# Reciprocals of the softmax sums by way of DRAM and GpSimd in the final stage of a transformer layer

## The reference, cut to what matters

```
probs = softmax(where(mask, -inf, q k^T / sqrt(32) + attention_bias))   # per head
ctx   = probs @ v                                # heads side by side: [tokens, 512]
x     = x + (ctx @ Wo + bo)
h     = layernorm(x) * g2 + beta2
x     = x + gelu2(h @ W1 + b1) @ W2 + b2         # gelu2(t) = t * sigmoid(1.702 t)
out   = rotate(x)                                # groups of 4 columns by angles theta, phi
```

## Time and profile before

| | us |
|---|---|
| median of 3 runs (3502.69 to 3505.73) | 3504.41 |
| the profiled execution: its time | 3502.99 |
| its span, first to last instruction | 3501.3 |
| its first two stages with their drain, to about | 2438 |
| its eight super-tiles, from 2476.05 to the end | 1025 |

### The profile page before, as it was taken

One profiled execution on the slowest core, in us unless ns is written; L12 is line 12 of the kernel. 1 busy time (PEld: TensorE's weight loads), 2 busy tenths in 40 slices (PEclk: granted clock), 3 DMA queues, 4 the chain that ended last, 5 costly groups with the idle time before them and its releaser, 6 DMA issues.

```text
span 3501.3 us, 60955 instructions
## 1 busy us (share of the span) xinstructions
PE 3415.7 (98%) x18338; PEld 1940.2 (55%) x18338; DVE 2486.0 (71%) x4176; ACT 1885.6 (54%) x2541; POOL 2084.9 (60%) x646
## 2 busy tenths in 40 slices
PE   8999799999999999999999999998899999999998
PEld 3444466666666666666666666665344444444443
DVE  5666599999999999999999999997434333343331
ACT  3222388888888888888888888886111111111110
POOL 0000499999899999999998999996202201211100
PEclk9999899999999999999999999999999999999999
DMA  8999999999999999999999999999402211210100
GB/s 290 340 338 339 360 365 349 344 348 351 399 344 348 350 350 345 394 352 349 351 343 367 378 351 347 346 351 324 107 19 54 72 32 40 72 51 21 48 12 12
DMA packets 288702, 906.20 MB, mean 259 GB/s; under 512 B 93344, under 2 KB 93344, under 8 KB 211360
## 3 DMA queue, kind: packets, MB, share of 16 engines
q1 hardware_dynamic: 240272, 811.43, 64.8%
q10 hardware_dynamic: 45840, 86.00, 7.0%
q0 software_dynamic: 2560, 8.39, 0.6%
HBM read 763.12 MB, written 142.61 MB: 259 GB/s over the span
## 4 chain that ended last, share of the span: by engine, by line
PE 86%; DVE 1%; DMA 1%; issue 0%; ACT 0%; SPq 0%; POOL 0%; DVEq 0%; ACTq 0%
PE b_T L765 27%; PE bank_ctx L788 14%; PE scores L731 14%; PE scores L1309 13%; PE b_T L1320 9%; PE bank_ctx L1320 3%; PE scores L1290 3%; PE scores L737 1%; DMA penb<-in_L_cond_b 1%; PE scores L1250 0%; PE scores L1299 0%; PE b_T L1326 0%; DVE probT L1151 0%; PE scores L1264 0%; ACT penb L1049 0%
## 5 line engine op out<-in xcount | busy, mean ns | idle before, releaser
L590 POOL TENSOR_TENSOR ring<-ring,penb 128x1856 f32<-128x1856 f32 x512 | 1904.5, 3759 | 502.1 <-DMA penb<-pen_scratch 416.8
L685 ACT ACTIVATE ring<-ring,low 128x2048 f32<-128x2048 f32 x512 | 1028.9, 2010 | 318.1 <-DVE low L654 318.1
L765 PEld LDWEIGHTS b_T<-ident,ring 128*128 128x128 f32 x8192 | 889.3, 141 | 434.2 <-DVE probT L638 430.8
L765 PE MATMUL b_T<-ident,ring 128*128 128x128 f32 x8192 | 1091.1, 276 | 6.5 <-DVE probT L638 5.9
L654 DVE CUSTOM_DVE_ANT_0 ring<-scores,ring 128x1024 f32<-128x1024 f32 x512 | 627.1, 1225 | 177.0 <-PE scores L731 153.8
L638 DVE COPY probT<-b_T 128x512 f32<-128x512 f32 x1024 | 702.0, 686 | 3.9 <-PE b_T L765 3.8
L654 DVE CUSTOM_DVE_ANT_0 ring<-scores,ring,low_part 128x1024 f32<-128x1024 f32 x512 | 652.6, 1275 | 0.4
L731 PE MATMUL scores<-keys,queries 128*128 (+1 forms) x2048 | 621.1, 424 | 21.1 <-DMA queries<-q_rows 16.7
L788 PE MATMUL bank_ctx<-probT,values 128*32 128x512 f32 x4096 | 546.2, 605 | 0.1
L695 ACT COPY probT<-b_T 128x512 f32<-128x512 f32 x1024 | 537.7, 575 | 0.2 <-PE b_T L765 0.2
L1016 POOL TENSOR_TENSOR keys_again<-keys_again,values 128x512 f32<-128x512 f32 x32 | 40.4, 1263 | 779.1 <-DVE values L1239 779.1
(11 more groups left out here) (131 smaller groups left out, 1930.9 us busy)
## 6 DMA issues: line engine op xcount, KB each, us to landing
ring<-in_fside_Bx16xSxS SPq DMA_DIRECT2D x512, 1024.0 KB, 7.4
keys<-k_rows SPq DMA_DIRECT2D x64, 1024.0 KB, 8.5
values<-v_heads ACTq DMA_DIRECT2D x128, 256.0 KB, 6.2
queries<-q_rows SPq DMA_DIRECT2D x128, 256.0 KB, 8.0
ctx_scratch<-ctxp ACTq DMA_DIRECT2D x128, 256.0 KB, 6.6
penb<-ctx_scratch SPq DMA_DIRECT2D x120, 256.0 KB, 4.7
k_rows<-part_hi SPq DMA_DIRECT2D x64, 256.0 KB, 3.3
k_rows<-part_lo SPq DMA_DIRECT2D x64, 256.0 KB, 3.4
```

Source lines behind the costliest of these rows:

```text
L590: nc.gpsimd.tensor_tensor(ring[:, j, 0:POOL_MASKED], ring[:, j, 0:POOL_MASKED], penb[:, j, 0:POOL_MASKED], ALU.add).then_inc(masked, 1)
L685: nc.scalar.activation(ring[:, k, :], ring[:, k, :], ACT.Exp, bias=low[:, k:k + 1], scale=-1.0, accum_out=column(sums_all, trip, k)).then_ ...
L765: last = nc.tensor.transpose(turn_bank(slot, n)[:, c * P:(c + 1) * P], ring[:, slot, at:at + P], ident[:])
```

## The change

From super-tile 1 on the reciprocals are no longer widened on ScalarE, turned on PE and multiplied on VectorE. All reciprocals of group 0 (super-tiles 0 and 1) are made before step 0 of the drain, those of the other three groups once, at `front(1, 1)`. PE turns them in 1 and 3 transposes, ScalarE copies the result over `low_all` and stores it to a new DRAM tensor `recip_scratch` (`keep_rows`). SP loads them with each piece as rows spread over 32 partitions each (`load_per_row`, one more DMA of 256 KB a piece), and GpSimd multiplies (`context`). GpSimd starts on super-tile 1 when the four tiles of super-tile 0 are normalised (`first_hn`). Super-tile 0 keeps the old way.

Beside that: bo is loaded in the place of g2, and g2 with beta2 and b2; VectorE waits for bo alone before the sums with it, and for the other rows after all four pieces and these sums; b2 is added to super-tile 0 at f = 2, 3, 9 and 13 of the first feed-forward; the three `sem_inc` stand ahead of `first_front`.

```diff
+        after(-1)
         for j in range(R):
             step(TRIPS, j)
             after(j)
...
+        def load_per_row(to, group, half, c, signal):
+            sp.dma_start(to, recip_scratch[bass.ds(group * H + 4 * c, 4), bass.ds(half * TOK, TOK)]
+                         .rearrange("h (o n) -> h o n", o=1).to_broadcast([4, DH, TOK])).then_inc(signal, 16)
...
-        sp.dma_start(g2_all, row(g2)).then_inc(vec_in, 16)
+        sp.dma_start(bo_all, row(bo)).then_inc(bo_in, 16)
...
         after_scores(7)
+        sp.dma_start(b2_all, row(b2)).then_inc(vec_in, 16)
+        sp.dma_start(g2_all, row(g2)).then_inc(vec_in, 16)
         sp.dma_start(beta2_all, row(beta2)).then_inc(vec_in, 16)
-        sp.dma_start(bo_all, row(bo)).then_inc(vec_in, 16)
-        sp.dma_start(b2_all, row(b2)).then_inc(vec_in, 16)
...
                 load_parts(parts[:, c % 2], v, c, part_ld[c % 2])
+                load_per_row(per_row[:, c % 2], v // 2, v % 2, c, part_ld[c % 2])
...
+        sp.wait_ge(recip_stored[0], 16)
+        load(1)
+        sp.wait_ge(recip_stored[1], 16)
+        with sp.Fori(2, NU) as v:
...
+        def context(v, c):
+            pool.wait_ge(part_ld[c % 2], (v - 1) * 160 + (c // 2) * 80 + 80)
             add_parts(parts[:, c % 2], v, c)
+            pool.wait_ge(summed, v * DB + c + 1)
+            if c == 0:
+                pool.wait_ge(wo_done, v * QT)
+            nc.gpsimd.tensor_tensor(ctxT[:, c, :], parts[:, c % 2, 0, :], per_row[:, c % 2], ALU.mult).then_inc(ctxT_ready, 1)
...
+        pool.wait_ge(first_hn, QT)
         for c in range(DB):
-            parts_of(1, c)
+            context(1, c)
...
+    def keep_rows(act, recip_rows, first, count, n):
+        act.wait_ge(recip_turned, n)
+        nc.scalar.copy(of_groups(low_all, first, count), recip_rows[:, first * GC:(first + count) * GC]).then_inc(recip_copied, 1)
+        act.wait_ge(recip_copied, n)
+        act.dma_start(recip_scratch[first * H:(first + count) * H, :].rearrange("(g h) (j q) -> (h j) g q", h=H, q=P),
+                      of_groups(low_all, first, count).rearrange("p (g q) -> p g q", q=P)).then_inc(recip_stored[n - 1], 16)
...
         if j == 3:
-            widen(act, 0, 2)
-            widen(act, 0, 3)
+            keep_rows(act, up[0], 0, 1, 1)
+            widen(act, 2)
+            widen(act, 3)
...
+            if isinstance(v, int) and v == 1 and f == 4:
+                keep_rows(act, fore[0], 1, GROUPS - 1, 2)
...
-            context(0)
-            context(1)
-            dve.wait_ge(vec_in, 80)
-            nc.vector.tensor_scalar(b1_scaled[:], b1_col[:], 1.702, None, ALU.mult).then_inc(consts_ready, 1)
+            for c in range(DB):
+                context(c)
+            dve.wait_ge(bo_in, 16)
             dve.wait_ge(xm_ld, 16)
-            for t in range(2):
-                nc.vector.tensor_tensor(xm_in[:, t, :], xm_in[:, t, :], bo_all, ALU.add)
-            context(2)
-            context(3)
-            for t in range(2, QT):
+            for t in range(QT):
                 last = nc.vector.tensor_tensor(xm_in[:, t, :], xm_in[:, t, :], bo_all, ALU.add)
             link(last)
+            dve.wait_ge(vec_in, 64)
+            nc.vector.tensor_scalar(b1_scaled[:], b1_col[:], 1.702, None, ALU.mult).then_inc(consts_ready, 1)
...
-            for t in range(QT):
-                last = nc.vector.tensor_tensor(x2[:, 0, t, :], x2[:, 0, t, :], b2_all, ALU.add)
-            link(last)
...
+            if isinstance(v, int) and v == 1 and f in (2, 3, 9, 13):
+                first_residual((2, 3, 9, 13).index(f))
+            if isinstance(v, int) and v == 1 and f == 1:
+                divisors(dve, fore[1], 1, GROUPS - 1, 2)
...
-        first_front()
-        dve.sem_inc(c_chain, LINKS - 1)
+        dve.sem_inc(c_chain, LINKS)
         dve.sem_inc(hid_ready, 4)
         dve.sem_inc(acc_read, 4)
+        first_front()
...
         def front(v, f):
-            if 1 <= f <= DB:
-                c = f - 1
-                pe.wait_ge(wide_ready, v * DB + c + 1)
-                if c < 2:
-                    need(pe, hT_ready, v * DB - 1 + c)
-                else:
-                    pe.wait_ge(ctxT_ready, v * DB + c - 1)
-                turn_recip(pe, v, c, fore[c % 2])
-            elif 5 <= f < 9:
+            if isinstance(v, int) and v == 1:
+                if f == 3:
+                    turn_recip(pe, fore[0], 1, GROUPS - 1, 2)
+                if f == 5:
+                    pe.wait_ge(recip_copied, 2)
+            if 5 <= f < 9:
```

More of the change, by code:

```diff
@@ L481, in __init__ @@
     def __init__(self, ring, penb, probT, keys, queries, values, scores, bankT, bank_ctx,
-                 masked, scored, added, turned, pv_done, ctx_copied, ctx_stored, SCORED0, TURNED0, PV0):
+                 masked, scored, added, exp_done, turned, pv_done, ctx_copied, ctx_stored, SCORED0, TURNED0, PV0):
         self.ring, self.penb, self.probT = ring, penb, probT
@@ L485, in __init__ @@
         self.scores, self.bankT, self.bank_ctx = scores, bankT, bank_ctx
-        self.masked, self.scored, self.added, self.turned = masked, scored, added, turned
+        self.masked, self.scored, self.added, self.exp_done, self.turned = masked, scored, added, exp_done, turned
         self.pv_done, self.ctx_copied, self.ctx_stored = pv_done, ctx_copied, ctx_stored
@@ L805, in phase_b, with phase_c @@
                     Left(ring, penb, probT, keys_again, queries_again, values, scores, bankT, bank_ctx,
-                         masked, scored, added, turned, pv_done, ctx_copied, ctx_stored, SCORED0, TURNED0, PV0))
-def phase_c(nc, sem, ctx, left, ctx_scratch, xm_scratch, Wo, bo, W1, b1, W2, b2, g2, beta2, out, ident, trig, sums_all, low_all):
+                         masked, scored, added, exp_done, turned, pv_done, ctx_copied, ctx_stored, SCORED0, TURNED0, PV0))
+def phase_c(nc, sem, ctx, left, ctx_scratch, xm_scratch, Wo, bo, W1, b1, W2, b2, g2, beta2, out, ident, trig, sums_all, low_all,
+            recip_scratch):
     CH = 2
@@ L1089, in scalar, with divisors @@
         supertiles(act, ffn, front, nothing)
[L1091 to L1096, removed]
+    def divisors(dve, undefined, first, count, n):
+        cols = slice(first * GC, (first + count) * GC)
+        sums = of_groups(sums_all, first, count)
+        nc.vector.tensor_scalar(undefined[:, cols], of_groups(low_all, first, count), 2.0, 0.0, ALU.mult, ALU.mult)
+        nc.vector.reciprocal(sums, sums).then_inc(recip_chain, 1)
+        dve.wait_ge(recip_chain, n)
+        nc.vector.tensor_tensor(sums, sums, undefined[:, cols], ALU.add).then_inc(recip_ready, 1)
     def vector_between(dve, j):
-        if j == 0:
-            divisors(dve, 0)
+        if j == -1:
+            dve.wait_ge(left.added, TRIPS * R * CH)
+            divisors(dve, fore[1], 0, 1, 1)
     def vector(dve):
-        LINKS = 7
+        LINKS = 6
         def first_front():
@@ L1174, in front @@
                     last = nc.vector.tensor_tensor(xm_in[:, t, :], xm_in[:, t, :], bo_all, ALU.add)
[L1175 removed]
+                link(last, 1)
             if 5 <= f < 9:
@@ L1184, in front @@
                     last = nc.vector.bn_stats(stats[:, t, :], x2_v[:, t, :])
-                link(last, 3)
+                link(last, 2)
                 dve.nop(nofuse=True)
@@ L1240, in late, with turn_recip @@
                 last.then_inc(rotated, 1)
[L1242 to L1243 removed]
+        dve.sem_inc(c_chain, LINKS)
         dve.sem_inc(hid_ready, 4)
         dve.sem_inc(acc_read, 4)
+        first_front()
         supertiles(dve, ffn, front, late)
[L1248 to L1250 removed]
+    def turn_recip(pe, recip_rows, first, count, n):
+        pe.wait_ge(recip_ready, n)
+        for g in range(first, first + count):
+            last = nc.tensor.transpose(recip_rows[:, g * GC:(g + 1) * GC], of_groups(sums_all, g, 1), ident[:])
         last.then_inc(recip_turned, 1)
     def tensor_between(pe, j):
+        if j == 2:
+            turn_recip(pe, up[0], 0, 1, 1)
         if j in (2, 4):
[L1256 removed]
+            if j == 4:
+                pe.wait_ge(recip_copied, 1)
             for c in (j - 2, j - 1):
                 pe.wait_ge(wide_ready, c + 1)
[L1259 removed]
+                for t in range(QT):
+                    last = nc.tensor.transpose(first_fore[c][:, t * P:(t + 1) * P], first_wide[:, c % 2, t, :], ident[:])
+                last.then_inc(wide_turned, 1)
     def tensor(pe):
```

84 lines of the change are left out of this document (37 added, 47 removed).

## The result

The changed kernel takes 3468.52 us (median of 4 runs, 3466.98 to 3469.0), the kernel before 3504.49 us: 36.0 us less, ratio 0.9897 with a 95% interval of 0.988 to 0.9914. The forecast was 3467 us. The profiled execution took 3466.98 us with a span of 3465.3 us, against 3502.99 and 3501.3.

What follows compares the result with a forecast made beforehand. PE was taken as the bound inside the super-tiles, a chain of loads, VectorE work and a semaphore at the join; 3502.99 - 23.3 - 14.1 = 3465.6 us, plus 1.4 for the runs' median, gave 3467 us, range 3461 to 3477.

Steps and rivals of the forecast that it cites:

- clock at the first up-products: First feed-forward stretch after PE's idle time: the 3.1 us loss to the lower clock stays, 0 change.
- Part 1: Super-tiles: 28 sets of reciprocal transposes (L1250) and PE's waits go, three transposes are added; 23.3 us less.
- Part 2: GpSimd's pieces are ready before PE's product with Wo at f = 5: 7.5 us ahead, 13 at super-tile 1; cost 0.
- two reloads of 5 to 6 us: Super-tile 1: two reloads, beside three GpSimd pieces of 5.3 us, bring GpSimd to about 2487, PE needing them at 2500.
- Part 3: Drain ends 3 to 4 us earlier; GpSimd's last sum, 2435.3, is late next; product with Wo over at 2439.5 to 2441.2.
- Part 4: Join: rows land at 2441.94 and release the first sum after Wo at 2442.2, not 2449.83; 7.6 us less.
- Part 5: End of preparation: sums with b2 leave the path, PE starts at 2461.95 behind ScalarE's copies; 6.5 us less.
- (a): Rival at the join: only part is gained, as W1 or rows land late or the drain ends no earlier; 3 to 10 us, chance 0.20.
- (b): Rival in the super-tiles: VectorE and GpSimd hold each other up, 7 to 14 us come back; chance 0.10.
- (c): Rival at f = 5 of seven super-tiles: GpSimd becomes the bound and the kernel slower, 3512 us or more; chance 0.03.
- (d): Rival: new waits replace those removed in the super-tiles and loads still bound the join; 3500 to 3508 us, chance 0.03.

Runs made afterwards that it cites:

- the loop alone: Changed kernel with the join put back as before (row loads, sums with b2, semaphore increments): 3479.81 us, 24.5 us below the kernel before.
- GpSimd's order: Changed kernel with GpSimd summing, and VectorE multiplying, super-tile 0's pieces in load order (0, 2, 1, 3): 3468.59 us.
- n = 3: Changed kernel with three extra GpSimd multiplications, results unused, in each piece of super-tiles 2 to 7: 3470.25 us.
- n = 6: Changed kernel with six extra GpSimd multiplications, results unused, in each piece of super-tiles 2 to 7: 3527.41 us.
- the two runs on the increments: Kernel before with the three semaphore increments moved ahead of super-tile 0's preparation: 3502.57 us; the same with GpSimd held back by the `first_hn` wait: 3499.76 us.
- the last kernel: Changed kernel with rows loaded ahead of W1, GpSimd's sums in load order, and W2's second half loaded behind super-tile 1's loads: 3463.7 us.
- the increments alone: Kernel before with only the three semaphore increments moved ahead of super-tile 0's preparation: 3502.57 us, ratio 0.9992.
- both orders: Changed kernel with rows b2, g2, beta2 loaded ahead of W1's first half and GpSimd's super-tile 0 sums in load order: 3468.18 us.

## Why the prediction was right

The forecast, 3467 us, missed by 1.5 us. Its terms, in the profiled executions:

| step | predicted | measured |
|---|---|---|
| sets of L1250 and their waits, less three transposes | 23.3 | 23.3 |
| clock at the first up-products | 0 | 1.1 |
| first sum after Wo | 7.6 | 5.15 |
| sums with b2 and the increments | 6.5 | 6.5 |
| sum | 37.4 | 36.0 |

The first row is 24.4 less 1.1. (Worked out without the clock: from the second super-tile's feed-forward to the last one's, six starts, they were 128.74 us apart on the mean and are 125.36. Seven times the difference, less 0.33 us for the three new transposes, is 23.4.) The 1.1: 16 matmuls of the first up-products took 9.87 us before, where 6.87 is their length at full clock, 3.0 us lost; now 24 took 12.24 in place of 10.3, 1.9 us lost. The third is 2449.83 less 2444.68 (7.6 was worked out from 2442.2); the fourth is 26.22 us from there to PE's start, before, less 19.74.

**Part 1** held to 0.1 us, and the loop alone shows it by itself (23.2 us behind PE's start): what stood in PE's own queue was won whole, and nothing took its place.

**Part 2** held for super-tiles 2 to 7: ready at T + 25.9, T + 26.9 foretold, 8.4 us to spare, 7.5 foretold. The run with 7.6 us of extra work stands just at the threshold, the one with 15.2 us far beyond it. For super-tile 1 its size was wrong: 13 us foretold, 1.9 us measured. The step that failed is "two reloads of 5 to 6 us": they took 10.3 and 11.8 us. The nearest row was a single DMA's landing (4.6 us), not that of five DMAs one after the other, 1.25 MB, of which the last has to land. The second also ran beside 1 MB of input rows. It cost nothing in this kernel, and 5.5 to 5.7 us in the two runs that changed GpSimd's order and left W2 where it was: 3.5 to 3.8 us of waiting, and 1.9 us of clock in the product behind.

**Part 3** was right on the drain (4.7 us earlier, 3 to 4 foretold) and on what is late next, GpSimd's last sum. But that sum ended at 2437.2, not 2435.3, so that the product started at 2438.05, not 2436.1, and I had 5.1 us as the product's worst, from the earlier trace rows; it took 6.6. A longer idle time isn't the reason: PE had stood 4.62 us before it, and 6.50 us in the kernel before, where it took 5.07. Over all 13 profiled executions the first 24 matmuls of this product took 10.54 us after 0.71, 1.74 and 2.96 us of idle time, and 11.9 to 13.6 us in the other ten, after 2.67 to 11.13 us. What decides between them isn't shown.

**Part 4** is the term that was mis-sized, 2.45 us too large. The rows landed at 2443.17, not 2441.94: the partial contexts, the first of the loads, were issued 2.1 us later in this execution (2404.77 for 2402.64), and the last of the rows 1.0 us later (2422.03 for 2421.05). The product with Wo, over at 2444.7, and not the rows, was the gate; rows put ahead by 2 MB gave 0.8 us, which is within the spread.

That this size is the kernel's own is not shown. The runs with extra work on GpSimd have the changed kernel's join as it is, since their extra work starts at super-tile 2. In the profiled execution with n = 3 the loads were issued from 2403.86 on, and the join came out as forecast (2442.2 and 2461.95), with the rows as the gate:

```profile
2441.86 0.18 DVE L1171 TENSOR_SCALAR b_scaled<-b_col 128x16 f32<-128x16 f32 x1 [3.06 <-DMA penb<-in_L_cond_beta]
2441.95 0.68 DVE L1174 TENSOR_TENSOR probT<-scores,penb 128x512 f32<-128x512 f32 x1
2461.69 13.48 PE L1345 MATMUL scores<-probT,ring 128*128 128x512 f32 x24 [1.50 <-ACT probT L1102]
```

With n = 6 PE's first up-product came at 2465.20. So one and the same join spreads over 3.5 us from one execution to the next, more than the forecast missed by; how near it came is in part luck.

**Part 5** held to 0.1 us, and from the first sum after Wo to PE's start it is 19.74 us with n = 3 as well. W1 was not the gate: its last load was issued at 2443.2 and landed 17.3 us later, 2460.5, 3.9 us before PE's start.

Of the rivals, (a) came to a small part, 2.45 us; (b) had no price in the super-tiles, but the two runs on the increments show its mechanism at the join, where VectorE's operations are on the path: 4.5 us on three operations. There the wait for `first_hn` keeps it off. In the changed kernel itself it was idle: the first load landed 7.0 us after the last tile was normalised. In the run with n = 3 it shows in the super-tiles too, on GpSimd's side (4.9 us for three multiplications, not 3.8), where it takes from the margin. (c) came true with 15 us more work per super-tile. (d) found nothing.

What is left open: how much of the last kernel's 4.8 us is its edits and how much the moment at which the first loads are issued, which differs by up to 5 us between the profiled executions of these kernels.

## What to carry to other kernels

Work that stands in the queue of the engine that is the bound is won in full (23.3 us foretold and measured here) when it is given to engines with slack; find the point where the receiving engine must be ready, and work out the margin there for the steady state and for the first round apart, since the first round has the loads against it. A move that only lets an engine finish early can be worth nothing: in the run of the loop alone TensorE then stood longer for the same load, and came back at the lower clock. Don't read a term of a few us off one profiled execution of a join: one and the same join came out 3.5 us apart in three executions. Two engines that slow each other are harmless until the overlap falls on the path, and a small shift elsewhere can put it there; a wait that keeps one of them back costs nothing if it has slack.

## What the runs showed of the hardware

- A GpSimd multiplication of 128x512 float32 took 1.27 us in the changed kernel (the 24 of super-tiles 2 to 7: 1.265 to 1.600), a VectorE one 0.69 us.
- Beside GpSimd, VectorE's 0.55 us operation took 2.12 us, though it reads a single tile from SBUF, and two of 0.69 us took 1.63 and 2.71 us; GpSimd's own took 2.78 for 2.34 us (the increments alone). Two of the three ended 0.3 and 0.55 us after the GpSimd operation beside them.
- After 4.6 us of idle time the granted clock was 0.50, and the first eight matmuls of the product took 6.6 us in place of 3.4; after 0.71 us it stayed at 1.00 (the last run); after 6.50 us they took 5.07 us (the kernel before), and after two waits of 7.5 us 5.2 and 6.7 us (n = 6). The length of the idle time alone doesn't tell what the next product takes: 24 matmuls took 10.54 us after 2.96 us and 12.23 us after 2.67 us (GpSimd's order, both orders).
- With several MB in the queue, a row of 256 KB landed 16 to 21 us after its issue (g2 16.1 and b2 20.9 in the kernel before); later, with little but these loads and 1 MB of input rows in the queue, a piece of five loads of 256 KB took 10.3 and 11.8 us.
